# The layer norm of a memory branch: late adds and statistics on VectorE, and early powers on GpSimd

## What is computed

```python
# _layernorm(x): (x - mean) / sqrt(var + 1e-5)
def _L1_xattn_ref(Z, kv, decay, W_in, b_in, W_out, b_out, gamma, beta):
    ...   # a decayed scan over kv, two projections, the mean over time
    summary = jnp.mean(proj, axis=1, keepdims=True)
    y = Z + summary
    mu = jnp.mean(y, axis=-1, keepdims=True)
    var = jnp.mean((y - mu) ** 2, axis=-1, keepdims=True)
    return (y - mu) / jnp.sqrt(var + LN_EPS) * gamma + beta

x = x + jnp.tanh(g_ffn[0]) * _L0_ffn_ref(_layernorm(x, axis=-1), ...)
x = x + jnp.tanh(g_xattn[1]) * _L1_xattn_ref(_layernorm(x, axis=-1), ctx_2048, ...)
x = x + jnp.tanh(g_ffn[1]) * _L1_ffn_ref(_layernorm(x, axis=-1), ...)
```

## Time and profile before

| what | value |
|---|---|
| median of 3 runs | 967.28 us (965.3 to 967.49) |
| the profiled execution's own time | 966.25 us |
| its span, first to last instruction | 964.4 us |
| granted TensorE clock, mean of the span | 0.874 |
| the memory stage in it: first L1301 to last L1035 | 292.82 to 343.93 us |
| the mixing stage: from the first L1047 on | 343.87 us |

### The profile page before, as it was taken

How to read it: one execution, slowest core, us unless ns; L and a number is a source line. 1 busy time by engine, 2 the same in 40 slices (tenths; PEclk the granted TensorE clock), 3 DMA queues, 4 the chain that set the end, 5 groups by cost and what they waited for, 6 DMA issues and landing times.

```text
span 964.4 us, 16889 instructions
## 1 busy us (share of the span) xinstructions
PE 793.1 (82%) x4572; PEld 512.1 (53%) x4572; DVE 619.4 (64%) x1467; ACT 427.7 (44%) x932; POOL 330.3 (34%) x598
## 2 busy tenths in 40 slices
PE   0599998988882268888879997999996989999990
PEld 0445554444441144658568875656664845666650
DVE  8488997678866757657522237378885777444445
ACT  0456666567760012223127765666664313333320
POOL 3000002235636542023855765200002484233340
PEclk9799999989996569555799997899999599999995
DMA  9410006999108960005444536200003122223217
GB/s 327 127 23 21 21 12 192 305 305 314 39 12 336 320 183 1 0 0 197 130 134 138 153 104 195 72 20 20 19 7 119 52 89 83 61 79 91 87 37 261
DMA packets 90278, 113.00 MB, mean 117 GB/s; under 512 B 11685, under 2 KB 81864, under 8 KB 89050
## 3 DMA queue, kind: packets, MB, share of 16 engines
q1 hardware_dynamic: 83434, 95.20, 32.6%
q0 software_dynamic: 6768, 16.86, 4.9%
HBM read 51.10 MB, written 58.42 MB: 114 GB/s over the span
## 4 chain that ended last, share of the span: by engine, by line
PE 60%; DVE 15%; issue 8%; ACT 7%; POOL 6%; DMA 2%; DVEq 1%; SPq 1%; POOLq 0%; ACTq 0%
PE ps L2084 9%; PE ps L1670 7%; PE ps L1660 6%; PE ps L2104 4%; PE ps L1975 4%; PE ps L1681 3%; POOL x_rows L547 3%; PE ps L1993 2%; PE ps L1968 2%; PE ps L1706 2%; PE ps L2051 2%; PE ps L1880 2%; PE ps L1893 2%; PE ps L1657 2%; PE ps L1693 1%
## 5 line engine op out<-in xcount | busy, mean ns | idle before, releaser
L769 ACT ACTIVATE probs_t<-ps 128x1024 f32<-128x1024 f32 x64 | 65.5, 1024 | 71.1 <-PE ps L1670 71.1
L611 POOL COPY work<-ctx_rows 128x256 f32 (+1 forms) x32 | 12.7, 399 | 212.1 <-PE ps L1681 212.1
L1149 DVE TENSOR_REDUCE row_max<-ps 128x8 f32<-128x1024 f32 x64 | 77.9, 1217 | 4.6 <-issue 2.4
L1155 DVE TENSOR_TENSOR work<-ps,row_max 128x1024 f32<-128x1024 f32 x64 | 77.7, 1214 | 3.4
L1512 DVE TENSOR_TENSOR ctx_cols<-ps,ctx_rows 128x512 f32<-128x512 f32 x54 | 37.3, 691 | 59.9 <-PE ps L2084 59.7
L1015 ACT ACTIVATE ctx_cols<-ctx_cols 128x256 f32<-128x256 f32 x54 | 22.5, 417 | 117.1 <-DVE ctx_cols L1512 117.1
L1670 PE MATMUL ps<-ident,work 128*128 128x128 f32 x512 | 70.0, 280 | 2.3 <-ACT work L763 2.1
L2084 PE MATMUL ps<-early,xt 128*128 x152 | 71.5, 593 | 0.0
L1670 PEld LDWEIGHTS ps<-ident,work 128*128 128x128 f32 x512 | 56.7, 142 | 17.3 <-ACT work L763 13.1
L588 POOL DMA_INDIRECT y_rows<-ctx_cols,w2d x38 | 37.5, 988 | 80.7 <-DMA y_rows<-ctx_cols,w2d 47.1
L2104 PE MATMUL ps<-early,ctx_cols 128*128 (+1 forms) x216 | 55.8, 381 | 4.2 <-ACT ctx_cols L1020 4.2
(11 more groups left out here) (331 smaller groups left out, 1977.5 us busy)
## 6 DMA issues: line engine op xcount, KB each, us to landing
x_rows<-pad_row SPq DMA_DIRECT2D x1, 17415.0 KB, 66.8
work<-x_rows SPq DMA_DIRECT2D x77, 129.0 KB, 2.1
x_rows<-pad_row SPq DMA_DIRECT2D x1, 7740.0 KB, 35.3
x_rows<-pad_row SPq DMA_DIRECT2D x1, 7611.0 KB, 92.2
early<-in_w3st SPq DMA_DIRECT2D x8, 512.0 KB, 6.2
work<-y_rows SPq DMA_DIRECT2D x16, 256.0 KB, 2.9
early<-y_rows SPq DMA_DIRECT2D x8, 512.0 KB, 7.3
late<-in_w2u SPq DMA_DIRECT2D x1, 2304.0 KB, 9.7
```

The costliest lines, as they stand in the source:

```text
L769: act.activation(probs_t[:, :, :], ps[:, 4:6, :], ACT.Copy).then_inc(sem("att.evac"), 1)
L1149: dve.tensor_reduce(row_max[:, u, 8 * c:8 * c + 8], scores(c), AX.X, ALU.max).then_inc(sem("att.max"), 1)
L1155: dve.tensor_tensor(probs[:, u, c, :].rearrange("p (h k) -> p h k", k=P), scores(c), row_max[:, u, 8 * c:8 * c + 8].unsqueeze(2).to_broadc ...
```

## The change

DVE's loop over pairs is written out, from t = 0 to t = 16 in steps of two. In round t it does step 1 of pair t, then step 4 of pair t-2, then bn_stats of `yb` of pair t and bn_stats of x of pair t-2, bn_aggr of both, step 3 of pair t, and last the copy of the statistics of pair t-2. For this the output of step 3 alternates between two buffers (`o_n` and `tmp[:, 1]`), `yst` has two halves, and `yb` has statistics of its own, `sty`. POOL's `dev2` of the first four pairs moves into the last two rounds of `ffn0`, which had no `dev1`; the other four come ahead of the first `beta`. `beta` is otherwise the same, and waits for a step 4 one pair earlier than before (`resid2` at t-2). Nothing is computed in another way, no DMA is touched, and no other stage is changed. On DVE, step 4 of a pair now stands right behind step 1 of the next pair, that is, where POOL's two adds L686 of that next pair begin.

```diff
+        yg = (o_n, tmp[:, 1])
+        yst = sb("yst", [P, 2, 2, 4])
+        sty = sb("sty", [P, 2, 6])
...
                 if t + 4 < NT:
                     dev1(t + 4, False, False)
+                else:
+                    for d in (2 * t - 24, 2 * t - 22):
+                        dev2(d, d == 0, False)
...
             def beta(t):
+                ys = yst[:, t // 2 % 2]
                 for u in range(2):
                     pool.wait_ge(sem("xn"), 2 * NT + t + u + 1)
                     TT(x[:, t + u, :], x[:, t + u, :], bet[:, :], ALU.add).then_inc(sem("mem.bet"), 1)
                 pool.wait_ge(sem("mem.aggr"), t + 2)
-                wait(pool, sem("resid2"), t)
+                wait(pool, sem("resid2"), t - 2)
...
+            for t in range(8, NT, 2):
+                dev2(t, False, False)
             pool.wait_ge(sem("dve.step"), 11)
-            dev2 = deviation(2)
-            dev2(0, True, False)
-            dev2(2, False, False)
             for t in range(0, NT, 2):
                 beta(t)
-                if t + 4 < NT:
-                    dev2(t + 4, False, False)
...
-            def memory(t, first, last):
+            def memory_in(t):
                 for u in range(2):
                     dve.wait_ge(sem("mem.sum"), t + u + 1)
                     dve.wait_ge(sem("ln.rstd"), 2 * NT + t + 2)
                     wait(dve, sem("mem.scaled"), t + u - 1)
+                    dve.scalar_tensor_tensor(yb[:, u], x[:, t + u, :], rstd[:, t + u:t + u + 1], bank(u, D), ALU.mult, ALU.add
                                              ).then_inc(sem("xn"), 1)
+            def memory_out(t):
                 for u in range(2):
                     dve.wait_ge(sem("mem.scaled"), t + u + 1)
                     dve.wait_ge(sem("mem.rstd"), t + 2)
+                    dve.scalar_tensor_tensor(x[:, t + u, :], yg[t // 2 % 2][:, u], yst[:, t // 2 % 2, u, 2:3], x[:, t + u, :],
+                                             ALU.mult, ALU.add).then_inc(sem("resid2"), 1)
+            for t in range(0, NT + 2, 2):
+                ys = yst[:, t // 2 % 2]
+                if t < NT:
+                    memory_in(t)
+                if t:
+                    memory_out(t - 2)
+                if t < NT:
+                    for u in range(2):
+                        dve.wait_ge(sem("xn"), 2 * NT + t + u + 1)
+                        dve.bn_stats(sty[:, u], yb[:, u]).then_inc(sem("mem.bn"), 1)
+                if t:
+                    for u in range(2):
+                        dve.wait_ge(sem("resid2"), t + u - 1)
+                        dve.bn_stats(st6[:, u], x[:, t - 2 + u, :]).then_inc(sem("bn"), 1)
+                if t < NT:
+                    wait(dve, sem("resid2"), t - 2)
+                    for u in range(2):
+                        dve.wait_ge(sem("mem.bn"), t + u + 1)
+                        dve.bn_aggr(ys[:, u, 0:2], sty[:, u]).then_inc(sem("mem.aggr"), 1)
+                if t:
+                    for u in range(2):
+                        dve.wait_ge(sem("bn"), 3 * NT + t + u - 1)
+                        dve.bn_aggr(mv2[:, u], st6[:, u]).then_inc(sem("bn.aggr"), 1)
+                if t < NT:
+                    for u in range(2):
+                        dve.wait_ge(sem("mem.aggr"), t + u + 1)
+                        dve.scalar_tensor_tensor(yg[t // 2 % 2][:, u], yb[:, u], ys[:, u, 0:1], gam[:, :], ALU.subtract, ALU.mult
+                                                 ).then_inc(sem("mem.scaled"), 1)
+                if t:
+                    keep_stats(3, t - 2)
```

More of the change, by code:

```diff
@@ L301, in build @@
         yb = tmp[:, 0]
-        yst = sb("yst", [P, 2, 8])
+        yg = (o_n, tmp[:, 1])
+        yst = sb("yst", [P, 2, 2, 4])
+        sty = sb("sty", [P, 2, 6])
         p_l2 = probs_t[:, 0, 0:2 * P].rearrange("p (s n) -> p s n", s=2)
@@ L672, in ffn0 @@
                     dev1(t + 4, False, False)
+                else:
+                    for d in (2 * t - 24, 2 * t - 22):
+                        dev2(d, d == 0, False)
+            dev2 = deviation(2)
             for t in range(0, NT, 2):
@@ L688, in beta @@
                 pool.wait_ge(sem("mem.aggr"), t + 2)
-                wait(pool, sem("resid2"), t)
-                TT(yst[:, :, 3], yst[:, :, 1], consts[:, 1:2].to_broadcast([P, 2]), ALU.add).then_inc(sem("mem.var"), 2)
+                wait(pool, sem("resid2"), t - 2)
+                TT(ys[:, :, 3], ys[:, :, 1], consts[:, 1:2].to_broadcast([P, 2]), ALU.add).then_inc(sem("mem.var"), 2)
                 pool.wait_ge(sem("mem.var"), t + 2)
-                TT(yst[:, :, 2], yst[:, :, 3], consts[:, 0:1].to_broadcast([P, 2]), ALU.pow).then_inc(sem("mem.rstd"), 2)
+                TT(ys[:, :, 2], ys[:, :, 3], consts[:, 0:1].to_broadcast([P, 2]), ALU.pow).then_inc(sem("mem.rstd"), 2)
+            for t in range(8, NT, 2):
+                dev2(t, False, False)
             pool.wait_ge(sem("dve.step"), 11)
-            dev2 = deviation(2)
-            dev2(0, True, False)
-            dev2(2, False, False)
             for t in range(0, NT, 2):
                 beta(t)
-                if t + 4 < NT:
-                    dev2(t + 4, False, False)
             for L in range(3, 6):
@@ L1300, in memory @@
                     wait(dve, sem("mem.scaled"), t + u - 1)
-                    dve.scalar_tensor_tensor(yb[:, u], x[:, t + u, :], rstd[:, bass.ds(t + u, 1)], bank(u, D), ALU.mult, ALU.add
+                    dve.scalar_tensor_tensor(yb[:, u], x[:, t + u, :], rstd[:, t + u:t + u + 1], bank(u, D), ALU.mult, ALU.add
                                              ).then_inc(sem("xn"), 1)
[L1303 to L1313, removed]
+            def memory_out(t):
                 for u in range(2):
```

## The result

The changed kernel takes 953.83 us (median of 4 runs, 950.82 to 957.51) where the kernel before, on the same chip, takes 966.29 (4 runs). The ratio is 0.987, 95% interval 0.983 to 0.991: 12.5 us less, between 8 and 16. Six later runs gave 953.32 us beside 966.23. One run of the kernel before, of 1023.6 us at a granted clock of 0.779, is left out of every median. Forecast were 959.8 us and a range from 954.5 to 964: the direction is right, the gain larger than the range allowed, by 0.7 us at its edge.

A forecast was written before the change was run, and what follows sets the result against it. DVE, with bubbles, was taken to bound the memory stage. Rounds of 4.25 + 0.76 = 5.0 us instead of 6.50, with a delayed start, end it 7.5 us earlier: 967.28 - 7.5 = 959.8 us, range 954.5 to 964.

The forecast's parts named there:

- The bound and the new round: Memory stage: the DVE-POOL chain is bound by DVE; its round falls from 6.50 to 5.0 us.
- the three reasons named: DVE's round: power made a round earlier (0.67 us), statistics not following their input (0.15), no branch or registers (0.55).
- The meeting: Step 4 and POOL's two adds delay each other on the shared SBUF port, costing 0.76 us a round.
- The start: First rounds: first L1301 stays at 292.82 us; four dev2 ahead of the first beta make DVE stand 2.7 us.
- The clock: Mixing behind the stage: clock rises as long after the stage's beginning as before; 2 us either side.
- starting point: Median of the kernel before, 967.28 us, from which the 7.5 us gain was subtracted.
- opposite of rival C: Stages behind: a longer stretch of full clock gives 950 to 955 us; chance 0.04.
- C: Mixing and attention: full-clock stretch from 356 to 390 us missed or broken off, 970.8 us; chance 0.06.
- B: Shared port: second step 4 precedes the waiting add, 956.6 us, or nothing blocks, 954.5; chance 0.15.
- D: Shared port: each instruction holds it for its whole length, 3.7 us more, 963.5 us; chance 0.12.
- A's round: Memory stage: the forecast's own round of 5.0 us, 959.8 us in all, range 957.5 to 962; chance 0.57.
- E: Memory stage: step 4 still waits for POOL each round, round above 6 us, 965 to 969 us; chance 0.06.

The follow-up runs named there:

- two kernels without the meeting: Changed kernel with POOL's early dev2 move undone, 950.40 us; changed kernel without POOL's two beta adds per pair, 947.17 us in a single run.
- DVE's part alone: DVE's new order with POOL's dev2 left where they stood before the change: 950.40 us, ratio 0.985.
- kernel 2 us later: Changed kernel plus six unused bn_stats, 2.1 us of DVE work, between memory stage and mixing: 959.31 us.

## Why the prediction was wrong, and where it was right

**The bound and the new round: right.** DVE sets the round, its bubbles go for the three reasons named, and the power is ready in time. The round was put at 4.25 + 0.76 = 5.01 us and is 4.02 + 0.76 = 4.78. The meeting was sized exactly, step by step (0.77 and 0.94 us for step 4, 0.90 for the second add, the first unchanged). The round without it was 0.23 us too long. The term that was mis-sized is bn_aggr and its surroundings: I took 0.2 us for each pair from the earlier trace rows, and four in a row now start 0.07 us apart (0.22 for one pair and the next pair 0.15 behind it), so both pairs cost 0.28 and not 0.4; the rest are some hundredths at each of the other steps. Over the five rounds from pair 4 to pair 14 it is 1.1 us.

**The start: right in kind.** POOL's four dev2 ahead of the first beta hold the first step 4 up: idle 3.4 us against 2.7 forecast, since DVE came to it sooner (the second step 1 ended at 294.71, 3.3 us after the first began; I had 3.7). Both early pairs of dev2 were hidden, as costed: in the profile after, dev2(4) and dev2(6) run from 284.4 to 286.7, with 1.64 us left ahead of L654. The first L1301 did not stay at 292.8 but came at 291.40, with the clock at full ahead of it. **The stage** was to gain 7.5 us and gained 8.9.

**The clock: the step that failed.** "2 us on either side are the price of a rise or a fall elsewhere by some microseconds." That the rise would come as long after the beginning as before was called an assumption; it came 5.6 us sooner, and the attention stage, for which I had nothing in the range, had 28.1 us at half clock instead of 42.5. The two together gave 6.3 us in the profiles, and 2.3 more came ahead of the stage, for which I had nothing either. In the medians the forecast was 6.0 us too high: 1.0 is its starting point (967.28 us from three runs, where the kernel before had 966.29 beside the result, which is the luck of few runs), 1.4 the stage, and 3.6 the clock's term, put at 0 with 2 us on either side. With the starting point and the stage right, 966.2 - 8.9 = 957.3, a range of 2 us on either side would still have missed the result; the term needed about 4. The table has medians from 3.8 us below to 2.3 above the mean, and two kernels 1.3 us apart in S were 6.0 apart in time. No step of the prediction had the clock rise sooner; only the 0.04 given to the opposite of rival C did.

**The rivals.** B (the port costs less) is refuted by the durations of step 4 and by the two kernels without the meeting. D (each holds the port for its whole instruction) too: the second step 4 ended 2.41 us after step 1 began, where D had 2.96 and the forecast 2.43. By the Trainium skill (SBUF — State Buffer, "Who interferes with whom"), with the lock held for the whole instruction, the round would have been 0.53 us longer, as estimated for D; the measurement decides for the shorter lock, and agrees with the page on who meets whom: step 1 and bn_stats, with one tile from SBUF, kept 0.86 and 0.74 us beside the adds (bn_stats in the kernel with DVE's part alone). C (the clock takes the gain back) did not come for this kernel. That the clock can take back a part is what the kernel 2 us later suggests, 6.0 us in the medians for 1.3 in S; the kernel with two more dev2 moved early does not show it cleanly, since its runs overlap the changed kernel's and its `ffn0` was held up as well. The opposite of C, 950 to 955 with a chance of 0.04, is the case that happened, beside A's round. E falls with the waits.

**What stays open** is what puts the clock's steps where they are. In the thirteen profiles of twelve kernels (the changed one has two) the rise came 5.6 to 6.2 us after the mixing's first matmul in seven and 11.0 to 11.6 us in six, and nothing between; the attention stage's share at half clock went from 14.7 of 45.7 us to 42.5 of 51.5. The length of the stage does not decide it (51.2, 48.4 and 40.6 us of stage gave 6 us, 49.1, 38.3 and 33.1 gave 11 to 12), nor does a full clock within the stage. Ahead of the stage the thirteen fall into two kinds as well: in five (the changed kernel's two among them) the clock stays at full up to the first step 1 and the thirteenth to the last residual add take 17.66 us (18.40 with the four dev2 in a row), in the other eight it is at half for a part of it and they take 19.35. That the changed kernel's remainder is low through the clock is what the table of single executions and the ten runs suggest; no run here sets the clock's steps and leaves the rest alone, so that another cause, such as where the program's code lies, is not excluded.

## What to carry to other kernels

When an engine's step is moved into the shadow of another's, look at what that other one is doing at that moment: here the new place met two adds on the shared port, 0.76 us a round, and the small operations that the change cleared away in front of those adds were what would have kept them apart. Time a change that shortens a stage by its own marks, first to last instruction, and expect the kernel's median to follow only within the scatter that the clock of the stages behind it brings (up to 4 us here); a change of that size can't be judged from the median of a few runs, unless time and clock are compared run by run. Ask also what a moved operation delays at its new place: four dev2 in a row held up an add ahead of the stage by 0.7 us. In a forecast, give every later stage whose clock changes level a term of its own.

## What the runs showed of the hardware

- Two instructions on the shared port do not exclude each other for their whole length. A DVE instruction with two SBUF inputs that waits for a POOL add runs its full 0.48 us from 0.19 us ahead of the add's end, and POOL's add goes in 0.15 us ahead of the DVE instruction's end. When both queue up they alternate; the one that has waited goes first (step 4 0.77, the second add 0.90, the second step 4 0.94 us in a round).
- Independent bn_aggr on DVE start 0.07 us apart, though each is shown with 0.14 to 0.16 us.
- In the thirteen profiles TensorE's granted clock went from 0.5 to 1.0 either 5.6 to 6.2 or 11.0 to 11.6 us after the mixing's first matmul, with PE equally busy before it (5.93 of 6.0 us and 11.28 of 11.6). A memory stage with mostly full clock, which fell 2 us before the mixing, had the late rise (11.6 us).
- The median of a kernel hides the clock of its runs: outside the changed stage, executions with 147 to 178 us at half clock took 907 to 911 us, those with 189 to 201 took 913 to 919.
